# VectorE's rounding of the next segment's tokens in four pieces, behind the division of q's recall

## The reference

```
xn  = layernorm(x)                       # per token
# a: attention over segments of 32 tokens, 16 heads of 64
q, k, v = split((xn * ln_g + ln_b) @ w_qkv)
for seg in 16 segments:                  # a scan; mem and z go from one to the next
    sdpa    = softmax(mask(rope(q) rope(k)^T * scale)) v
    mem_out = elu1(q) mem / (elu1(q) z + 1e-6)          # q's recall
    out     = beta * mem_out + (1 - beta) * sdpa
    prev_v  = elu1(k) mem / (elu1(k) z)                 # k's recall
    mem, z  = mem + elu1(k)^T (v - prev_v), z + sum(elu1(k))
# b: a linear layer in simulated fp8
xq = fake_quant_fp8(xn); wq = fake_quant_fp8(weight)
x = xn + a(out @ w_out) + xq @ wq^T + bias
```

## Time and profile before

| what | value |
|---|---|
| median of three runs | 3094.67 us (3094.19 to 3098.59) |
| the profiled execution | 3102.11 us |
| its span, first to last instruction | 3100.2 us |
| scan, first to last of its full steps | about 1700 to 3065 us |
| busy in the span: PE, DVE, ACT, POOL | 86%, 81%, 60%, 57% |
| mean granted TensorE clock | 0.939 |

### The profile page before, as it was taken

One profiled execution on the slowest core, in us unless ns is written; L12 is line 12 of the kernel. 1 busy time (PEld: TensorE's weight loads), 2 busy tenths in 40 slices (PEclk: granted clock), 3 DMA queues, 4 the chain that ended last, 5 costly groups with the idle time before them and its releaser, 6 DMA issues. The chain is left out here.

```text
span 3100.2 us, 127998 instructions
## 1 busy us (share of the span) xinstructions
PE 2652.2 (86%) x53041; PEld 1472.6 (48%) x53041; DVE 2513.5 (81%) x7598; ACT 1875.5 (60%) x3797; POOL 1760.1 (57%) x1988
## 2 busy tenths in 40 slices
PE   5887999999999999772431899999999999999998
PEld 2442333333333333372220566666666666666665
DVE  4678999999998999586606789888888888888887
ACT  5786999999999999630001455545455555555553
POOL 5883222222222222240063788888888888888886
PEclk9997999999999999995655999999999999999999
DMA  4676444444434443191023000000000000000000
GB/s 128 204 241 159 93 90 93 98 101 95 93 94 99 94 95 87 41 322 57 0 45 95 4 11 11 11 4 11 11 11 11 11 11 11 11 11 5 11 8 11
DMA packets 173628, 201.48 MB, mean 65 GB/s; under 512 B 31153, under 2 KB 134513, under 8 KB 172785
## 3 DMA queue, kind: packets, MB, share of 16 engines
q1 hardware_dynamic: 170480, 191.87, 24.0%
q0 software_dynamic: 2560, 1.35, 0.4%
HBM read 125.10 MB, written 67.24 MB: 62 GB/s over the span
## 5 line engine op out<-in xcount | busy, mean ns | idle before, releaser
L851 ACT ACTIVATE at_pA<-at_ps 128x512 f32<-128x512 f32 x1024 | 552.0, 615 | 55.3 <-DVE at_ps L903 48.8
L912 DVE CUSTOM_DVE_ANT_0 at_junk<-at_ps,w_cmask 128x512 f32<-128x512 f32 (+3 forms) x1024 | 463.2, 485 | 100.1 <-PE at_ps L754 92.5
L903 DVE TENSOR_TENSOR at_ps<-at_ps,w_ratio 128x128 f32<-128x128 f32 (+3 forms) x1024 | 450.9, 491 | 2.0 <-PE at_ps L748 0.5
L720 POOL TENSOR_SCALAR_AFFINE_SELECT at_pB<-at_pB 128x128 f32<-128x128 f32 x256 | 74.8, 292 | 637.1 <-ACT at_pB L857 634.9
L857 ACT ACTIVATE at_pB<-at_ps 128x512 f32<-128x512 f32 (+1 forms) x768 | 379.9, 532 | 52.5 <-PE at_ps L761 47.3
L2001 POOL TENSOR_TENSOR sc_rb<-sc_rb,v_sin 128x512 f32<-128x512 f32 x256 | 326.1, 1274 | 43.8 <-DVE sc_ra L2244 42.6
L2037 PE MATMUL sc_ps<-sc_xT,v_wqkv 128*128 128x512 f32 x512 | 287.6, 645 | 3.3 <-PEq L56 1.4
L748 PE MATMUL at_ps<-at_aq,at_ak 72*128 72x512 bf16 x1024 | 277.7, 387 | 0.7 <-DVE at_mx L912 0.4
L2201 ACT COPY sc_skN<-sc_ps 128x512 f32<-128x512 f32 x128 | 74.9, 586 | 320.3 <-PE sc_ps L2092 320.3
L761 PE MATMUL at_ps<-at_bq,at_bk 75*128 75x512 bf16 (+3 forms) x1024 | 265.5, 302 | 1.5 <-ACT at_pB L857 0.9
L1996 POOL TENSOR_TENSOR sc_sk<-sc_ee,sc_relu 128x512 f32<-128x512 f32 x128 | 164.8, 1288 | 172.3 <-ACT sc_ee L2192 172.3
(11 more groups left out here) (317 smaller groups left out, 5910.6 us busy)
## 6 DMA issues: line engine op xcount, KB each, us to landing
parts_scratch<-fr_parts SPq DMA_DIRECT2D x64, 384.0 KB, 4.1
at_bk<-parts_scratch SPq DMA_DIRECT2D x192, 96.0 KB
at_ak<-parts_scratch SPq DMA_DIRECT2D x192, 96.0 KB
v_scratch<-fr_v SPq DMA_DIRECT2D x32, 352.0 KB, 4.4
at_v<-v_scratch SPq DMA_DIRECT2D x32, 352.0 KB, 3.5
at_bq<-parts_scratch SPq DMA_DIRECT2D x128, 64.0 KB
at_aq<-parts_scratch SPq DMA_DIRECT2D x128, 64.0 KB
on_scratch<-at_on SPq DMA_DIRECT2D x32, 256.0 KB, 2.2
```

What stands on the lines that cost most here:

```text
L851: act.activation(pA[:, n % A_RING, j * S:(j + 1) * S], src, ACT.Exp).then_inc(exped, 1)
L903: dve.tensor_tensor(src[:, 0:wide], src[:, 0:wide], W["ratio"][:, S - wide:S], ALU.mult).then_inc(tilted, 1)
L912: ins = dve.tensor_tensor_reduce(junk[:, P * j * (j + 1) // 2:P * (j + 1) * (j + 2) // 2], src[:, col:col + wide], W["cmask"][:, S - wide: ...
```

## The change

round_fp8 at step 5 gives way to round_piece with k = 0 to 3, the same four instructions on the same tiles: k = 0 (the exponent's bits) at step 4, k = 1 (clamp and scale) and k = 2 (add) at step 5, k = 3 (subtract, into xq) at step 6. They stand behind the division of q's recall and ahead of k's rope, and moments at step 1 moves to the same place. shifts stays where it was. The opening segment, in prepare, still uses round_fp8.

```
+        def round_piece(dve, link, n, k):
+            v, m = flat(tq[:]), flat(mq[:])
+            if k == 0:
+                wait(dve, "tq_d", n)
+                link(dve.tensor_scalar(m.bitcast(I32), v.bitcast(I32), 0x7F800000, None, ALU.bitwise_and))
+            elif k == 1:
+                link(dve.tensor_scalar(m, m, Q_LEAST, Q_ROUND, ALU.max, ALU.mult))
+            elif k == 2:
+                link(dve.tensor_tensor(v, v, m, ALU.add))
+            else:
+                wait(dve, "xqt", n - 1)
+                dve.tensor_tensor(flat(xq[:]), v, m, ALU.subtract).then_inc(G["xq_d"], 1)
...
-                        for j in at_step(s, 1):
-                            moments(dve, link, j)
                         for j in at_step(s, 2):
                             shifts(dve, j)
-                        for j in at_step(s, 5):
-                            round_fp8(dve, link, j)
                         p = s - 2
                         if inside(p):
                             wait(dve, "qr_s", p + 1)
...
                             dve.tensor_tensor(by_head(t2[:, p % 2]), recalled[:, :, :, 0:DH], bc(head(rq[:]), DH), ALU.mult).then_inc(G["qd"], 1)
+                        for j in at_step(s, 1):
+                            moments(dve, link, j)
+                        for off, k in ((4, 0), (5, 1), (5, 2), (6, 3)):
+                            for j in at_step(s, off):
+                                round_piece(dve, link, j, k)
                         if s < PT:
                             rope(2 * s + 1)
```

## The result

The changed kernel takes 3134.26 us (median of 6 runs, 3131.55 to 3143.15) against 3096.52 us before (6 runs, 3091.3 to 3102.04). The ratio is 1.0124 with a 95% interval of 1.0111 to 1.0136: slower by 38 us, where 21 were forecast. The direction and the kind of loss were right, its size was too small.

The account below looks back on a forecast made before the run. DVE's stretch from L2300 to L2312, which PE's local awaits, was taken to bound. Costs of 4.55 a segment against 2.8 now, less 0.35, left 1.4, 21 us over 15: from 3094.67 to 3116 us, range 3086 to 3140.

Parts of the forecast that it names:

- The loop and its slack: From L2300 to L2312 DVE has next to no slack; PE's local follows by 0.15. Ahead of L2300, DVE usually waits 0.95.
- The stall's new place: PE's update no longer waits for L2303; PE's local waits for L2312 instead, four times a segment.
- Moments: Step 1: costs about 0.6 us now, 1.6 when moved between L2303 and "pt", including 0.1 for meeting POOL.
- length less 0.95: Pricing rule: DVE work ahead of L2300 costs its length less 0.95 us, DVE's usual wait there.
- Piece 0: Step 4: takes 0.65 us, sometimes waiting for POOL's L1996; turn_y covers 0.2, leaving a cost of 0.45.
- Pieces 1 and 2: Step 5: POOL's L1996 gets in between, so 2.1 us instead of 1.15; turn_x covers 0.2, cost 1.9.
- Piece 3: Step 6: takes 0.7 us, POOL having caught up; turn_xq covers 0.1 and does not wait; cost 0.6.
- What PE's idle gives back: PE's "issue" idles absorb 0.15 to 0.2 us of each wait at local; two more waits give back 0.35 a segment.
- its sign: In the new profile, a segment of 87 to 88 us would show the forecast right.

Follow-up runs that it names:

- e5: Kernel before with one needless reduction added in every step, ahead of the division of q's recall; ratio 1.0082, 25 us slower than before.
- e6: Kernel before with the same needless reduction in every step, but behind the division of q's recall; ratio 1.0173, 54 us slower than before.
- e2: Changed kernel with moments put back ahead of shifts, only the four pieces staying behind the division; ratio 1.0082, 25 us slower than before.
- e3: Changed kernel with the pieces at the same steps but ahead of the division, moments ahead too; ratio 0.9947, 16 us faster than before.
- e9: Changed kernel with one piece a step at steps 4 to 7, pieces and moments ahead of the division, turn_xq at step 8; ratio 0.9916, median 3076.76 us.
- e11: e9 with the pieces moved behind the division and nothing else; ratio 1.0027, 8 us slower than before.
- e12: e9 with moments cut in two, bn_stats at step 0 and the rest at step 1; ratio 0.9925 to before.
- e4: Changed kernel with one piece a step at steps 4 to 7, turn_xq at step 7, all still behind the division; ratio 1.0062, 19 us slower than before.
- e8: Changed kernel with one piece a step at steps 4 to 7, between "pt" and the memory's update, moments ahead, turn_xq at step 7; ratio 1.0126, 39 us slower.
- e7: Changed kernel with one piece a step at steps 4 to 7, pieces and moments ahead of the division, turn_xq at step 7; ratio 0.9948, 16 us faster.

## Why the prediction was nearly right, and where its sum was off

*The loop and its slack.* Right. Local follows "pt", work behind L2303 costs, work ahead of the division is largely covered. e5 and e6, and the pairs of e2 and e3 and of e9 and e11, show it.

*The stall's new place.* Half right. The update's wait went as forecast. But of the four waits a segment that I put at local, only step 1's is there (15 of the 18 waits, 28.0 of the 33.9 us); those of steps 4 to 6 stand at q's projection, for k's rope (3.1, 20.2 and 7.9 of the 31.2 us). The prediction named that wait for step 5 and then still took 0.2 off for turn_y and turn_x and 0.1 for turn_xq.

*Moments.* This is the term that was most in error, and on the side that is removed. I charged it 0.6 now. Step 1 takes 10.47 before, among neighbours of 10.24 and 10.42, and e12 gains nothing by halving it: by these it costs some 0.2 now, not 0.6. Behind the division it put "pt" 1.76 later (1.50, and 0.26 of waiting for POOL in L1845), where I had 1.6. So step 1 grew by 1.63, not by 1.0. The rule "length less 0.95" was too harsh near its edge: L2303 itself has some 0.2 of slack before PE's update, which starts 0.25 behind it in a plain step and 0.05 behind it where PE waited. That PE swallows part of what is left is argued, not shown.

*Piece 0.* It put "pt" 0.69 later, as the 0.65 taken; step 4 grew by 0.18, less than the 0.45. In e2 and e4, with the same piece in the same step, it grew by 0.47 and 0.46, so the 0.18 may well be chance.

*Pieces 1 and 2.* The mechanism, POOL in the gap, was right, and the size near: "pt" came 1.91 later in step 5, forecast 2.1. But it is a mean of two kinds: 1.2 in the six segments where POOL stayed out, and 2.4 in the nine where it got in. The instruction forecast, L1996, did so in three of them; in six it was L2016, which the prediction had as the extreme. That the mean is close to 2.1 is in part luck. The step took 12.54 against 12.55, so nothing was won there; forecast was 0.3.

*Piece 3.* Under-sized. It put "pt" 0.93 later, not 0.7, since POOL held it up in six of the 15 segments, where I had taken POOL to have caught up; nothing covered it, and PE's turn_xq waited for it five times (2.5 us), which I had excluded. Step 6 grew by 1.16 instead of 0.6.

*What PE's idle gives back.* The reduction behind the division had 0.19 a step swallowed, as the 0.15 to 0.2 taken. In the change, the 0.35 off the difference was not there in steps 1 and 6; the steps without moved work are 0.3 shorter together, which is within what such steps differ by, and whether PE's idles gave it back is not shown.

Added up: 1.0 + 0.45 - 0.3 + 0.6 - 0.35 gave 1.4 a segment; measured are 1.63 + 0.18 - 0.01 + 1.16 - 0.3, 2.64 with rounding. Moments (0.6) and piece 3 (0.6) are the difference; what was too low for pieces 1 and 2 and too high for piece 0 cancels. The segment came to 88.76, above the 87 to 88 that the forecast named as its sign.

## What to carry to other kernels

Before work is moved along an in-order engine, find the two signals between which it goes, and which of them another engine waits for last: here the idle that could have held the work stood ahead of the division, and the place behind it had none. Price what is moved at both ends by the measured length of its old step, not by a rule of slack, since what was hidden before comes back at nearly its full length. And follow every consumer past the move: a wait that one edit makes can sit in another instruction of the waiting engine, as k's rope did for q's projection and xq for turn_xq.

## What the hardware showed that was not expected

After long waits TensorE's granted clock fell from the higher of its levels, 2.4 GHz, to the lower, 1.2 GHz. A window of the changed kernel, and PE's timeline there:

```profile
2162.40:2165.80 3.40, 3.40 (x71) 2.40 (x72) 3.07 (x8) 0.00 (x0) 3.40 (x4) 0.50 0.02 5
```

```profile
2161.23 1.10 PE L2087 MATMUL sc_ps<-v_uu,sc_pT 32*32 32x64 f32 x64 [1.71 <-DVE sc_sm L2326]
2162.26 1.95 PE L2059 MATMUL sc_ps<-v_wqkv,sc_xT 128*128 128x256 f32 x4
```

After an idle of 1.71 in a step 1, the values took 1.95 at a granted clock of 0.50; 1.13 is usual. Not every long idle did it: of PE's 22 idles above 1.3 us in the changed kernel's 14 segments, ten have such a stretch at them or right behind them, of the seven before three, of the 15 in e8 thirteen. Of the changed kernel's 14 segments, seven have a mean granted clock below 1.00, of the kernel before three, of e8 thirteen, of e3, e7 and e9 none. In the changed kernel those seven average 89.26 us and the others 88.26, before 87.41 and 85.77. So, by an estimate from these, about 7 us (seven by 1.0) of the changed kernel's time and 5 us (three by 1.64) of the one before go with the lower level; the segments may differ in their waits too, so what the clock costs by itself is not shown. Most of the loss is not the clock's: 2.49 of the 2.64 us a segment stand between segments at full clock.
